# A four-layer graph network on one core: the column flags stored in runs of eight, and the masks of two tiles built at once

## What is computed

```python
def gat_layer(x, graph, W, b):
    h = x @ W
    s = jnp.einsum('bnd,bmd->bnm', h, h) * graph
    s = jnp.where(s == 0.0, NEG_INF, s)
    a = jax.nn.softmax(s, axis=2)
    return jnp.einsum('bnm,bmd->bnd', a, h) + b

heads = jax.vmap(lambda W, b: gat_layer(flow_x, graph, W, b))(Wh, bh)
cat = jnp.moveaxis(heads, 0, 2).reshape(B, N, H * D)
x = jax.nn.leaky_relu(cat, negative_slope=0.01)
out = gat_layer(x, graph, W_out, b_out)
```

## Time and profile before

| | us |
|---|---|
| runs | 2540.32, 2543.6, 2553.97 |
| the profiled execution | 2546.85 |
| its span, first to last instruction | 2545.1 |
| busy: TensorE, VectorE, ScalarE, GpSimd | 2136.4, 2120.1, 1429.5, 821.1 |
| granted TensorE clock, mean | 0.922 of full speed |

### The profile page before, as it was taken

The page is one execution under the profiler, slowest core; times in us unless marked ns, Lnnn a source line. Parts: engine busy times, 40 slices in busy tenths (PEclk is TensorE's granted clock), DMA queues, the critical chain, the costliest instruction groups (busy, mean ns, idle before and its releaser), DMA issues.

```text
span 2545.1 us, 59821 instructions
## 1 busy us (share of the span) xinstructions
PE 2136.4 (84%) x25470; PEld 1417.1 (56%) x25470; DVE 2120.1 (83%) x2864; ACT 1429.5 (56%) x2318; POOL 821.1 (32%) x473
## 2 busy tenths in 40 slices
PE   2868778467767669998998999999999989998886
PEld 1644446345546556665665665666656656655554
DVE  7558864778864539999997999999989989989996
ACT  2522222288962226666665666666666666665664
POOL 0039960000000013443443444444444444432221
PEclk8969999689988859999999999999999999999988
DMA  3000000000000032102121121121211211112562
GB/s 114 1 1 0 0 0 1 1 1 1 1 2 1 1 84 47 35 27 52 35 46 24 36 56 25 42 52 35 47 26 41 48 23 43 32 39 47 80 68 43
DMA packets 137246, 79.86 MB, mean 31 GB/s; under 512 B 123928, under 2 KB 125080, under 8 KB 136608
## 3 DMA queue, kind: packets, MB, share of 16 engines
q1 hardware_dynamic: 136992, 76.16, 13.5%
HBM read 67.44 MB, written 8.70 MB: 30 GB/s over the span
## 4 chain that ended last, share of the span: by engine, by line
PE 46%; DVE 8%; issue 5%; ACT 3%; another core or an unknown queue 1%; POOL 0%; DMA 0%; SPq 0%; POOLq 0%; DVEq 0%; ACTq 0%
PE ps_low L610 19%; PE ps_score L590 17%; PE ps_low L622 4%; DVE x_sb L721 4%; PE ps_low L638 2%; ACT hid_z L814 2%; DVE hid_masks L707 2%; DVE hid_weights_t L730 2%; PE ps_low L575 2%; PE ps_low L554 1%; DVE hid_xs L693 0%; PE ps_low L562 0%; DMA hid_bias<-in_bh_t 0%; PE ps_low L630 0%
## 5 line engine op out<-in xcount | busy, mean ns | idle before, releaser
L806 ACT ACTIVATE x_sb<-x_sb,hid_neg_max 128x1024 f32<-128x1024 f32 x576 | 661.3, 1153 | 314.2 <-DVE hid_neg_max L721 314.2
L730 DVE STREAM_TRANSPOSE hid_weights_t<-x_sb 128x1024 f32<-128x1024 f32 x576 | 709.2, 1232 | 1.9 <-ACT x_sb L806 1.3
L721 DVE CUSTOM_DVE_ANT_0 x_sb<-ps_score,adj_mask,row_scale 128x1024 f32<-128x1024 f32 x512 | 636.4, 1243 | 75.5 <-PE ps_score L590 56.2
L610 PE MATMUL ps_low<-hid_weights_t,hid_x_rep 32*64 32x256 f32 x18432 | 594.6, 386 | 31.0 <-issue 23.1
L590 PE MATMUL ps_score<-hid_y_hi,hid_xs 128*128 128x512 f32 x1152 | 528.3, 459 | 37.1 <-DVE hid_neg_max L721 31.9
L610 PEld LDWEIGHTS ps_low<-hid_weights_t,hid_x_rep 32*64 32x64 f32 x18432 | 398.4, 133 | 200.3 <-issue 131.5
L590 PE MATMUL ps_score<-hid_y_lo,hid_xs 128*128 128x512 f32 x1152 | 461.8, 401 | 0.0
L907 POOL TENSOR_TENSOR hid_z<-hid_z,hid_inv_cols 128x1024 f32<-128x1024 f32 x64 | 193.4, 3022 | 597.8 <-ACT hid_z L814 597.8
L590 PEld LDWEIGHTS ps_score<-hid_y_hi,hid_xs 128*128 128x128 f32 x1152 | 220.4, 191 | 268.1 <-issue 160.8
L590 PEld LDWEIGHTS ps_score<-hid_y_lo,hid_xs 128*128 128x128 f32 x1152 | 221.8, 193 | 44.9 <-issue 15.2
L899 POOL TENSOR_TENSOR hid_y_wide<-hid_y_wide,hid_y_hi 128x1024 f32<-128x1024 f32 x64 | 153.5, 2399 | 198.8 <-ACT hid_y_wide L797 198.8
(11 more groups left out here) (298 smaller groups left out, 3217.3 us busy)
## 6 DMA issues: line engine op xcount, KB each, us to landing
hid_inv_cols<-hid_inv_rows SPq DMA_DIRECT2D x64, 512.0 KB, 3.8
hid_x_rep<-hid_row_space SPq DMA_DIRECT2D x64, 256.0 KB, 5.9
adj_rows<-in_adj SPq DMA_DIRECT2D x8, 512.0 KB
marks<-hid_mark_rows SPq DMA_DIRECT2D x8, 512.0 KB, 5.4
x_sb<-in_x SPq DMA_DIRECT2D x2, 1024.0 KB, 6.2
x_saved<-x_sb SPq DMA_DIRECT2D x1, 2048.0 KB, 8.4
hid_row_space<-h_sb SPq DMA_DIRECT2D x8, 256.0 KB, 4.6
hid_row_space<-hid_shifted SPq DMA_DIRECT2D x8, 256.0 KB, 9.4
```

The source lines that it names most:

```text
L610: ins = pe.matmul(m.ps_low[c * F:(c + 1) * F, a, 0:NT * Q], x_rep[a * Q:(a + 1) * Q, batch_of(g) % 2, b, :], weights_t[a * Q:(a + 1) * Q, ...
L721: dve.tensor_tensor_reduce(ring[:, i % RING, :], m.ps_score[:, i % 2, :], mask, scale, HUGE, ALU.add, ALU.min, neg_max[:, g % 2, t:t + 1]) ...
L730: dve.transpose(weights_t[:, g % 2, :, t, :], ring[:, i % RING, :].rearrange("p (b j) -> p b j", j=Q)).then_inc(tile_turned, 1)
L806: act.activation(ring[:, i % RING, :], ring[:, i % RING, :], ACT.Exp, scale=-1.0, bias=neg_max[:, g % 2, t:t + 1], accum_out=row_sum[:, g ...
```

## The change

`store_flags` writes `col_rows[b]` as it lies in SBUF: 128 pieces of 8 flags, 16 B each. The flags in DRAM are then in the order (p, t). `spread_flags` reads them in that order into a new tile `col_wide`, 2 KB per partition as before, and waits for `col_cast`, the copy of the batch before, where it waited for the masks of the batch before the last. A new ScalarE instruction per batch, `order_flags`, in the unit before the batch's own, after the exponential of tile 2, copies `col_wide` into `col_mask` with p and t exchanged (128 x 1024 bf16, reading at a step of 16 B). `build_mask` runs in every second step, for the tiles i+4 and i+5 together: 128 x 2048, with `col_mask` read twice through a step of zero in the outer dimension. `masks` has four places where it had two.

```diff
-        masks = sb("masks", [P, 2, N], BF16)
+        masks = sb("masks", [P, 4, N], BF16)
+        col_wide = sb("col_wide", [P, P, NT], BF16)
-        col_rows = nc.dram_tensor("hid_col_rows", (B, N), BF16).ap()
+        col_rows = nc.dram_tensor("hid_col_rows", (B, P, NT), BF16).ap()
@@ SyncE
             def store_flags(b):
                 sp.wait_ge(flags_ready, 2 * b + 2)
-                sp.dma_start(col_rows[b].rearrange("(t p) -> p t", p=P), col_flag[:, b, :],
-                             allow_slow_non_contiguous=True).then_inc(col_stored, 16)
+                sp.dma_start(col_rows[b], col_flag[:, b, :]).then_inc(col_stored, 16)
             def spread_flags(b):
                 sp.wait_ge(col_stored, 16 * (b + 1))
-                if b >= 2:
-                    sp.wait_ge(mask_built, (b - 1) * NT)
                 if b:
-                    sp.wait_ge(col_spread, 16 * b)
-                sp.dma_start(col_mask[:, b % 2, :],
-                             col_rows[b].rearrange("(a n) -> a n", a=1).to_broadcast([P, N]))\
+                    sp.wait_ge(col_cast, b)
+                sp.dma_start(col_wide[:].rearrange("p i t -> p (i t)"),
+                             col_rows[b].rearrange("(a p) t -> a (p t)", a=1).to_broadcast([P, N]))\
                     .then_inc(col_spread, 16)
@@ VectorE
             def build_mask(i):
                 b, t = i // NT - HEAD_UNITS, i % NT
                 if t == 0:
-                    dve.wait_ge(col_spread, 16 * (b + 1))
-                if i >= HEAD_UNITS * NT + 2:
-                    dve.wait_ge(masked_ready, i - 1)
-                dve.tensor_tensor(masks[:, t % 2, :], m.mask[:, t, :], col_mask[:, b % 2, :], ALU.min)\
-                   .then_inc(mask_built, 1)
+                    dve.wait_ge(col_cast, b + 1)
+                if i >= HEAD_UNITS * NT + 4:
+                    dve.wait_ge(masked_ready, i - 2)
+                dve.tensor_tensor(masks[:, t % 4:t % 4 + 2, :], m.mask[:, t:t + 2, :],
+                                  col_mask[:, b % 2, :].unsqueeze(1).to_broadcast([P, 2, N]), ALU.min)\
+                   .then_inc(mask_built, 2)
-                    mask, scale = masks[:, t % 2, :], row_flag[:, b, t:t + 1]
+                    mask, scale = masks[:, t % 4, :], row_flag[:, b, t:t + 1]
-                    if HEAD_UNITS * NT <= i + 3 < TILES:
-                        build_mask(i + 3)
+                    if t % 2 == 0 and HEAD_UNITS * NT <= i + 4 < TILES:
+                        build_mask(i + 4)
@@ ScalarE
+            def order_flags(b):
+                act.wait_ge(col_spread, 16 * (b + 1))
+                if b >= 2:
+                    act.wait_ge(mask_built, (b - 1) * NT)
+                act.copy(col_mask[:, b % 2, :].rearrange("p (t i) -> p t i", t=NT),
+                         col_wide[:].rearrange("p i t -> p t i")).then_inc(col_cast, 1)
+                    if t == 2 and HEAD_UNITS <= g + 1 < UNITS:
+                        order_flags(g + 1 - HEAD_UNITS)
```

More of the change, by code:

```diff
@@ L415, in last_attention @@
         col_spread = sem("col_spread")
+        col_cast = sem("col_cast")
         mask_built = sem("mask_built")
```

## The result

Four runs of the changed kernel took 2468.56 to 2475.01 us, median 2469.83; the kernel before, 2547.78 in the same comparison. The ratio is 0.970, with an interval of 0.967 to 0.973, and the medians differ by 78 us. The profiled execution of the changed kernel took 2475.01, the slowest of its four, with a span of 2473.3. The forecast was 2474.

The account below looks back on a forecast made before the run. TensorE and VectorE were both full in the units before the last eight, VectorE bound those; 2546.85 - 65.2 (flag store) - 2.2 (merged builds) - 5 (fewer GpSimd meetings) = 2474.4, said as 2474 us, range 2463 to 2509.

Parts of the forecast that it names:

- The bound: Plain and row-turning units: TensorE and VectorE both full, so any stop adds time; last eight units: VectorE, 24.97 of 25.00 us.
- The flag store: Store issued once per batch: 128 pieces of 16 B instead of 1024 remove all stalls in its eight units, 65.2 us.
- The prediction's other reading: Flag store: 16 B pieces are still read-modify-write, only eight times fewer, so 8 us of stall stay; time 2482.
- tiny writes are completed slowly: Flag store: 2 B writes into DRAM are handed over quickly but complete slowly, stalling 5 to 13 us where it happens.
- The step from the store to TensorE: Units with a flag store: TensorE's instructions, also fetched from DRAM, come behind the tiny writes; called an inference.
- The mask build: VectorE, last eight units: 32 double builds save 2.2 us, fewer meetings with GpSimd 5 us (bounds 0 to 15.4).
- The order copy: Eight new ScalarE copies, 1043 ns each if like the nearest row; costed at nothing, bounds 0 and 17 us.
- The waits: Changed waits of spread_flags, order_flags and the build: the queue is no later, cost nothing.
- Stalls that stay: Rival at the flag store: the row save directly ahead blocks, not the 2 B pieces; 2540 us, chance 0.08.
- half of them: Rival at the flag store: 16 B is still small, half the excess, 33 us, remains; 2507 us, chance 0.08.
- One element at a time: Rival at the merged mask build: packed rate lost, 32.6 us of loss; 2509 us, chance 0.05.
- ScalarE late for the spread: Rival in units 63 to 70: ScalarE stands before order_flags for a late spread, 11 us each; 2562 us, chance 0.02.

Follow-up runs that it names:

- three kernels: Changed kernel with extra transfers in even units 12 to 60, varying piece size, form or distance in turn: 2545.17, 2583.17 and 2519.41 us.
- the fourth kernel: Changed kernel with, in even units 12 to 60, a load behind nothing, behind meeting 2 B pieces or behind pieces 512 B apart: 2542.02 us.

## Why the prediction was right, point by point

**The bound** was read rightly: in the head units both TensorE and VectorE are full, and every stall was added whole. What the flag stores cost was taken as 59.0 us in the seven head units; the stretch shrank by 61.4. The missing 2.4 us are in five plain units of the kernel before that lie one or two units behind a flag store and took 20.1 to 20.8 us instead of 19.9, which I had not counted. Two of them (20.80 and 20.38) lie behind the fourth store: it was not free, as the prediction had it, but cost 1.3 us. (The granted clock was 0.84 in three of the long units and 0.85 in a fourth, not 0.84 in four.) The prediction's "nothing is caught up" was true, and a little more was lost.

**The flag store.** All of it went, as the sum took it: 21.24 us where 31 to 34 had been. The control rows carried this: the 32 B stores and the row saves. The prediction's other reading started from the Trainium skill, "DMA: Bandwidth & Descriptors", section Specifications: transfers under 512 B are done by read-modify-write. An eighth of the stall would then be left, and the time be 2482 us. As a price of the stall this is not borne out: 1024 pieces of 16 B and 1024 of 2 B that lie apart stall nothing. My own reading of the cause, "tiny writes are completed slowly", was right only in half. It is the writes that meet in a short stretch which complete slowly; 1024 pieces of 16 B, as many as before, stall nothing either. Why meeting writes are slow, no run shows.

**The step from the store to TensorE** was called an inference and is still one in its last part. What the runs show: a load behind such a store completes some 13 us late; a stall comes back in nearly every unit in which such a store is put; and its length goes largely with the unit. In units 22 and 42 the extra stores of 2 B pieces added 13.5, 13.7, 14.4 and 9.2, 15.2, 16.1 us, in units 12, 32 and 52 between 3 and 8, in three kernels; in the fourth kernel unit 32 grew by 1.4 only. And unit 35, with the fourth flag store, is longer in neither of the two kernels that write it in 2 B pieces. What is the same in these kernels is every engine's row of instructions, and so where the fetches of a unit fall. That fits waits for instructions, but is no proof, and a store in another queue, or one behind which the instructions had been fetched already, was not tried.

**The mask build** was costed at 0.07 us a pair, 2.2 us, and at 5 us from fewer meetings with GpSimd. The packed rate held (1224 ns; I had 0.60 + 0.53 us from start to start), and the waits behind GpSimd fell from 15.4 us to 49.7 - 32 x 1.224 = 10.5. Of these 7.1 us the tail shows 4.4 between the kernel with the store alone and the changed one. With the eighth stall, 6.15 idle us, the forecast for the tail was 13.35 and it shrank by 12.85. The prediction took a build behind GpSimd to need its own full time after it; it ended 0.55 us after L894 and takes 0.68 in the clear, so a little less is lost.

**The order copy** takes 2094 ns, twice the row it was costed from, which was the upper bound. It cost nothing, and its double cost nothing.

**The waits** that changed hands moved nothing: the spreads are issued earlier in their units, and no transfer is later.

**The rivals.** Stalls that stay, or half of them: none stayed. One element at a time: not so. ScalarE late for the spread: no such wait. The sum was 72.4 us; the spans differ by 71.8, of which 2.5 are lost ahead of the last layer in that one execution.

**Where it was luck.** That the sum is met within 1 us is luck. By one profile of each kernel the store was worth more than the 65.2 us of the sum, 61.4 in the head units and 230.22 - 221.77 = 8.45 in the tail, 69.9 together; the build less than 7.2, 4.4. The two misses, 4.7 us too little and 2.8 too much, and the 2.5 us lost ahead of the layer all but cancel. And the stalls differ from one execution and chip to the next: the runs of the kernel before reach from 2531.34 to 2553.97 us. By medians the gain is 69 to 78 us.

## What to carry to other kernels

Before costing a small store by its bytes, look at what the engines do in the 20 us behind it: here 2 KB per batch cost 8 us each time, on engines that have nothing to do with it, under waits that the profile names only "issue" or "remote", or puts down to an engine that stood as well. Cut the trace at a regular event, such as one store per unit, and compare the lengths; a unit that stands out by 10 us then names its cause by what is issued in it. And when a two-input instruction on a bounding VectorE must share SBUF with GpSimd, move it by one step and look which of the two waits; here that gave 8 us of 2473.

## What was not expected of the hardware

- 128 pieces of 2 B, written side by side into 256 B of DRAM, complete 19.4 us after their issue; the same pieces 16 B apart, 3.5 us; and 1024 of them side by side, in the one unit that shows it, within 18.7 us. 1024 pieces of 2 B that lie 512 B apart stall nothing.
- Pieces of 4 B side by side add 3 to 7 us to a unit, pieces of 16 B side by side nothing.
- A load of 4 KB issued 0.5 us behind such a store completes after 15 to 19 us, where it takes 3.2 to 4.8 otherwise.
- A ScalarE copy of 128x1024 bf16 that reads at a step of 16 B takes 2094 ns; a copy of 1024 f32 elements side by side took 1043. Whether the step or the two-byte type makes the difference was not tried.
